# A first mixture layer whose last bias is added outside its products, with two dense token tiles in place of three, and blank products and earlier tables in the last layer

## The chip, the cores and the metric

The kernel runs on one core of a Trainium2 chip. The metric is the device time of one execution in microseconds (us). Three runs of the kernel before took 1397.26, 1397.58 and 1397.50 us, a median of 1397.5. The core has TensorE (PE in the profile; its weight loads are PEld), VectorE (DVE), ScalarE (ACT), GpSimd (POOL) and SyncE (SP), which issues most DMAs.

## The reference, cut to what matters

2048 tokens of 128 floats (8 sequences of 256, 16 tiles of 128 tokens) go through four pairs of an attention-like stage and a mixture-of-experts stage, with a layer norm after each. Two mixtures matter here. The first has 8 experts, and each token takes its 2 best:

```
gout = xt @ Wg.T; topv, topi = top_k(gout, 2); w = softmax(topv)
g = xt @ W1[e].T + b1[e];  v = xt @ W2[e].T + b2[e];  h = silu(g) * v       # 128 -> 256
eo = h @ W3[e].T + b3[e]                                                    # 256 -> 128
out = sum over e of comb[t, e] * eo[e, t];   x = layernorm(x + out)
```

The last runs four times over the tokens with one pool of 16 experts; each token takes one expert per round (`router` differs by round), and the result of a round is the input of the next:

```
logits = xt @ router; w = max(softmax(logits)); idx = argmax(logits)
out[t] = w[t] * (silu(xt[t] @ W1[idx[t]]) @ W2[idx[t]])                      # 128 -> 512 -> 128
```

All data is fp32. The bias `b3` takes part as the sum over e of `comb[t, e] * b3[e]`.

## The kernel before, in words

The program is a row of blocks, one per stage; each block has an instruction list for each engine, written out by hand in order, and semaphores (`Tally` counts) between them. A stage begins on all engines together when the one before is over on all of them. The order inside a queue is the order of the code.

**The first mixture, `moe_l0_stage` (L862), from 192 to 350 us of the span.** Its parts follow one another:

- SP issues the loads of all weights (L921, L922), of b3 (L923, one row of 8 x 128) and of the filters of the next stage. DVE finds each token's two experts, their weights, and for each (token, expert) pair a row in a buffer in DRAM that is sorted by expert. The first `DENSE` = 3 token tiles are left out of this; the other `SORTED` = 13 are sorted. DVE also builds `table`, which says for each of `PAIR_TILES` = 33 tiles of 128 pair rows where its expert's weights and bias lie and where its rows begin. It makes it by a diagonal that PE multiplies by ones (L985), and DVE casts the result (L1164, L1165).
- POOL scatters the sorted tokens into the pair rows: 2 x `SORTED` indirect DMAs (L966), one after the other.
- Meanwhile the three dense tiles go through all 8 experts (PE from L991, ACT L1058, DVE L1180 and L1188). A unit u is half of an expert's hidden width: two products with 384 columns (L994), `silu` on ACT, the gate on DVE (`m_inner`). After both halves PE makes, for each of the three tiles, a bias product (`k.ones[0:1]` by a row of b3, L1003) and two products with W3 into the same bank (L1005); DVE adds the result, scaled by `comb`, to `k.X`. PE has the sums of expert e behind the first half of expert e+1.
- SP waits until every scatter has landed (L926) and for the table, then loads pair tiles, up to `XRING` = 12 ahead (L934). Between them it issues four large zero fills of the last layer's row buffers (`clear_rows`, L1826, 2448 KB each), behind the 6th, 12th, 18th and 24th tile.
- The pair loop over 33 tiles. PE in step v: turns tile v (L1019); makes the 4 up products of tile v-1 (L1027); reads two registers from `table` (L1032 and L1034), and makes for tile v-3 the bias product (L1039) and two down products (L1041). ACT: reads a register (L1065), picks the expert's up weights of tile v (`m_up`, L1070) once `m_hT` of tile v-2 is made, two `silu` of tile v-1 (L1077), and writes tile v-3 out scaled (`m_ys`, L1085). DVE: copies the turned tile v (L1199), its destinations (L1202), then `m_hT` of tile v-2 (L1210). POOL scatters each tile to the two sums in DRAM (L972).
- SP loads the sums back in four groups (L941), and DVE adds both to `k.X` (L1219).

**The last mixture, `moe_l3_stage` (L1848), from 1025 us.** DVE finds the experts (L2149 on); PE starts with products of two "fold" banks (L1987), then counts (L2001 to L2003), and later the remaining banks; the folds turn W2 and the later routers into one matrix. POOL makes constants first (L1931 to L1947), then scatters 16 tiles (L1953). A round is a loop over 31 tiles like the pair loop. At its end PE makes `totals` (L2057), DVE `list_tiles` (L2113 on), PE spreads the table (`spread_table`, L1993), and SP begins to load the next round's tiles. At the start of each layer norm and of the first mixture PE runs 8 products of `k.blank` by the identity, 512 columns each (L126, L978), into a bank that nobody reads.

## Time and profile before

| | |
|---|---|
| Median of three runs | 1397.5 us |
| The profiled execution, its own time | 1397.07 us |
| Its span | 1395.3 us |
| Mean granted clock of TensorE | 0.87 of full speed |
| PE / PEld / DVE / ACT / POOL busy | 80% / 59% / 59% / 39% / 25% |
| DMA | 135.02 MB, mean 97 GB/s |

The span is the stretch from the first to the last instruction; the time has 1.8 us around it. A busy share says how long an engine had work in flight, not that it set the pace. In the timeline rows below, the first number is the start in us from the span's start, the second the time to the end of the last of the merged instructions, then engine, line, operation, output and inputs, the count, and in brackets the idle time before it and what ended that. Matmuls are pipelined: for their cost one reads from start to start. Each fp32 matmul has two records or more. In the rows of windows "PEclk" is the granted clock, 1.00 for 2.4 GHz and 0.50 for 1.2 GHz.

### The profile page before, as it was taken

How to read it: one execution, taken by the hardware profiler on the slowest of the kernel's cores; microseconds unless marked ns; L12 is line 12 of the kernel's file. 1: busy time of each engine (PE TensorE's matmuls, PEld its weight loads, DVE VectorE, ACT ScalarE, POOL GpSimd, SP SyncE). 2: the span in 40 equal slices, each digit the busy share in tenths (PEclk: the TensorE clock that was granted, in tenths of full speed). 3: DMA queues.
4: the chain of work that ended last, by engine and by line, in shares of the span. 5: the costliest groups of instructions: out<-in, count | busy, mean ns of one | idle time of the engine just before them, and what ended most of it. 6: DMA issues, size and time to landing. Idle time of an engine off the chain costs nothing. (4 is left out here: it accounts for less than half of the span.)

```text
span 1395.3 us, 31629 instructions
## 1 busy us (share of the span) xinstructions
PE 1111.8 (80%) x10680; PEld 817.0 (59%) x10680; DVE 823.7 (59%) x2873; ACT 546.6 (39%) x1175; POOL 343.3 (25%) x471
## 2 busy tenths in 40 slices
PE   8999889886887544789976856987698979789791
PEld 4655546775454531456644424553678969789791
DVE  6566163333588897745566885546853656656334
ACT  4456522454432001222222114322115757667581
POOL 3344325133100000000000015540033424424351
PEclk9999999998988557799997966999877989989896
DMA  2200646452000019238217065553902212021222
GB/s 52 53 25 3 241 171 248 159 196 67 1 3 3 4 37 374 85 82 177 38 40 257 2 201 133 145 114 124 301 21 64 56 35 59 24 65 44 50 52 62
DMA packets 112351, 135.02 MB, mean 97 GB/s; under 512 B 16795, under 2 KB 78316, under 8 KB 111539
## 3 DMA queue, kind: packets, MB, share of 16 engines
q1 hardware_dynamic: 99730, 118.48, 27.6%
q0 software_dynamic: 12464, 14.53, 4.1%
q8 instruction: 90, 1.47, 0.4%
q14 instruction: 67, 0.54, 0.1%
HBM read 67.13 MB, written 69.06 MB: 98 GB/s over the span
## 5 line engine op out<-in xcount | busy, mean ns | idle before, releaser
L2044 PE MATMUL m_psY<-large,m_hT 128*128 x992 | 141.5, 286 | 0.2
L2030 PE MATMUL m_psH<-m_xT,m_up 128*128 128x128 f32 x992 | 139.3, 286 | 0.0
L2030 PEld LDWEIGHTS m_psH<-m_xT,m_up 128*128 128x128 f32 x992 | 129.3, 203 | 0.0
L2044 PEld LDWEIGHTS m_psY<-large,m_hT 128*128 128x128 f32 x992 | 129.0, 194 | 0.5 <-issue 0.3
L1970 POOL DMA_INDIRECT rows<-m_ys,m_slot x93 | 90.5, 973 | 132.1 <-DVE m_slot L2238 119.7
L567 DVE TENSOR_REDUCE at_peaks<-at_ps 128x3 f32<-128x384 f32 x128 | 65.4, 551 | 47.8 <-PE at_ps L330 47.8
L2087 ACT ACTIVATE m_up<-large 128x512 f32 x124 | 78.0, 629 | 29.5 <-DVE m_valid L2141 17.2
L479 ACT ACTIVATE at_PT<-at_ps,at_bias 128x384 f32<-128x384 f32 x128 | 67.3, 577 | 50.3 <-PE at_ps L340 50.2
L1445 POOL IOTA sl_late<- 64x1024 f32 x2 | 2.0, 984 | 331.1 <-POOLq L682 331.1
L2096 ACT ACTIVATE m_hT<-m_psH 128x512 f32<-128x512 f32 x124 | 73.2, 590 | 20.6 <-PE m_psH L2030 20.4
L126 PE MATMUL ln_idle<-blank,ident 128*128 128x512 f32 x112 | 53.7, 635 | 26.2 <-PEq L883 13.5
L274 POOL TENSOR_SCALAR_AFFINE_SELECT at_PT<-at_PT 128x256 f32<-128x256 f32 x128 | 54.9, 430 | 74.1 <-ACT at_PT L479 70.2
L2108 ACT ACTIVATE m_ys<-m_psY,m_weight 128x144 f32<-128x144 f32 x124 | 47.3, 381 | 34.8 <-PE m_psY L2044 33.1
L126 PEld LDWEIGHTS ln_idle<-blank,ident 128*128 128x128 f32 x112 | 22.3, 205 | 53.2 <-issue 53.2
L972 POOL DMA_INDIRECT pair_sums<-m_ys,m_dest x33 | 32.4, 983 | 72.0 <-DVE m_dest L1202 55.0
L2019 PE MATMUL m_psX<-ident,m_xs 128*128 128x128 f32 x124 | 38.6, 311 | 14.3 <-DMA m_xs<-rows 13.0
L327 PE MATMUL at_ps<-large,at_QA 32*128 32x256 f32 x256 | 46.4, 437 | 3.5 <-ACT at_PT L479 2.3
L1342 ACT ACTIVATE pe_sg<-pe_psG 128x512 f32<-128x512 f32 x36 | 21.5, 597 | 69.6 <-PE pe_psU L1310 69.6
L1318 PEld LDWEIGHTS pe_psD<-m_wd,pe_hid 128*128 128x128 f32 x288 | 37.5, 191 | 18.7 <-DVE pe_hid L1363 13.8
L1664 PE MATMUL m_acc<-se_place,se_parts 128*128 128x512 bf16 x192 | 47.1, 399 | 0.0
L337 PE MATMUL at_ps<-at_QA,large 32*128 32x256 f32 x256 | 44.8, 425 | 2.5 <-ACT at_PT L479 2.3
L1357 DVE TENSOR_TENSOR pe_hu<-pe_psU,pe_sg 128x512 f32<-128x512 f32 x32 | 22.1, 691 | 35.8 <-ACT pe_sg L1342 35.8
(662 smaller groups left out, 2682.7 us busy)
## 6 DMA issues: line engine op xcount, KB each, us to landing
rows<-blank SPq DMA_DIRECT2D x16, 2448.0 KB, 15.2
m_xs<-rows SPq DMA_DIRECT2D x124, 76.5 KB, 1.9
pair_rows<-blank SPq DMA_DIRECT2D x1, 8320.0 KB, 25.8
large<-in_L_attn_firs SPq DMA_DIRECT2D x4, 2048.0 KB, 18.0
large<-comb_rows SPq DMA_DIRECT2D x64, 128.0 KB, 4.9
se_wu<-in_L_ffn_up SPq DMA_DIRECT2D x32, 192.0 KB, 2.6
W2T<-in_L_ffn_down_turned SPq DMA_DIRECT2D x1, 4096.0 KB, 12.6
large<-in_L_ffn_up SPq DMA_DIRECT2D x4, 1024.0 KB, 8.1
```

The lines of the kernel that those rows point to most:

```text
L126: nc.tensor.matmul(idle[:], k.ident[:], k.blank[:, 0:512], start=True, stop=True)
L274: nc.gpsimd.affine_select(out=diag(PT[:, v % PRING]), in_=diag(PT[:, v % PRING]), compare_op=ALU.is_ge, fill=0.0, base=0, pattern=[[0, 2], ...
L327: return nc.tensor.matmul(psS[:, u % TILES, P:CAUSAL], QA[rows, g, keys(b, 1)], KA[rows, g, b * SEQ:(b + 1) * SEQ], start=False, stop=True ...
L479: nc.scalar.activation(PT[:, v % PRING, :, :].rearrange("p x c -> p (x c)"), psT[:, v % TRING, 0:CAUSAL], ACT.Exp, bias=k.at_bias[:, v % H ...
L567: nc.vector.tensor_reduce(peaks[:, b % 2, n, :], psS[:, u % TILES, 0:CAUSAL].rearrange("p (x c) -> p x c", c=P), AX.X, ALU.max).then_inc(r ...
L1664: i = nc.tensor.matmul(acc[:, g, :], parts[:, j // 2 % 2, part, :], place[:, j // 2 % 2, g * 512:(g + 1) * 512], start=False, stop=True, s ...
L1970: pool.indirect_dma_start(k.rows[(layer + 1) % 2], bass.IndirectOffsetOnAxis(slot[:, q:q + 1], 0), ys[:, q, :], None, bounds_check=E3 * N ...
L2030: m = nc.tensor.matmul(psH[b][:, c * P:(c + 1) * P], up[b][:, c * P:(c + 1) * P], xT[b][:], start=True, stop=True)
L2044: m = nc.tensor.matmul(psY[b][:, 0:wide], hT[b][:, c * P:(c + 1) * P], k.W2[:, bass.ds(e + c * WIDE, wide)], start=(c == 0), stop=(c == C ...
L2087: nc.scalar.activation(up[b][:], k.W1[:, bass.ds(e, F3)], ACT.Copy).then_inc(picked.sem, 1)
L2096: nc.scalar.activation(hT[b][:], psH[b][:], ACT.Silu).then_inc(silu_done.sem, 1)
L2108: nc.scalar.activation(ys[:, q, 0:WIDE], psY[b][:, 0:WIDE], ACT.Copy, scale=weight[:, j % XRING:j % XRING + 1]).then_inc(y_out.sem, 1)
```

## The change

In the first mixture:

- `DENSE` is 2 and `SORTED` 14. The dense units have 256 columns, the pair tiles are 35, the scatters 28.
- The bias products (L1003, L1039) and the register reads for them (L1034) are gone; the down products start their banks themselves. `table` has three parts.
- b3 is laid out on the host as a [128, 1024] matrix: row (half, tile of 8, expert), column (tile of 8, d), b3 where both tiles are the same and zero elsewhere. Its load has 512 KB in place of 4 KB.
- `comb` holds all 16 tiles. PE turns it behind unit 1, ACT copies it out, and behind units 5, 8, 11 and 14 PE makes a product of 64 rows by 512 columns, whose result is the bias sum of four token tiles; DVE adds it to `k.X`. ACT's and DVE's copies of X for the scatter are waited for first.
- ACT runs a one-column `silu` behind the `exp`, before it waits for the weights.

In the last mixture:

- POOL makes two constants that DVE made, ahead of its other work; DVE starts its search on the logits in place of a copy, and copies them later, while it would wait for the counts.
- ACT runs a one-column `silu` behind the folds.
- PE runs 5 blank products (512 columns) behind the last fold bank, and between rounds 5 behind `totals` and 6 behind the spread table.

```diff
-DENSE = 3
+DENSE = 2
@@ moe_l0_stage
-    GROUPS = [range(DENSE, DENSE + 4)] + [range(t, t + 3) for t in range(DENSE + 4, T, 3)]
+    OFFERS = (5, 8, 11, 14)
+    GROUPS = [range(2, 6), range(6, 10), range(10, 13), range(13, 16)]
-        b3 = sb("b3", [1, E * D])
+        b3 = sb("b3", [P, 8 * D])
@@ block.tensor
                     for t in range(DENSE):
                         o = sums_of[d % 2][:, t * P:(t + 1) * P]
-                        nc.tensor.matmul(o, k.ones[0:1, :], b3[0:1, d * D:(d + 1) * D], start=True, stop=False)
                         for h in range(C):
                             m = nc.tensor.matmul(o, inner[:, (2 * d + h) % 4, t * P:(t + 1) * P],
-                                                 W3[...], start=False, stop=h == C - 1)
+                                                 W3[...], start=h == 0, stop=h == C - 1)
                     m.then_inc(summed.sem, 1)
+                if u == 1:
+                    pe.wait_ge(*mixed.at(1))
+                    nc.tensor.transpose(psC[:, 0:P], flat(comb), k.ident[:]).then_inc(mix_turned.sem, 1)
+                if u in OFFERS:
+                    g = OFFERS.index(u)
+                    pe.wait_ge(*mix_out.at(1))
+                    if g:
+                        pe.wait_ge(*taken.at(g))
+                    rows = slice(64 * (g // 2), 64 * (g // 2) + 64)
+                    nc.tensor.matmul(psC[:], combT[rows, :], b3[rows, g % 2 * 512:(g % 2 + 1) * 512],
+                                     start=True, stop=True).then_inc(offered.sem, 1)
...
-                    pe.reg_load(bias[j % 4], table[0:1, 2 * NT + j:2 * NT + j + 1])
-                    d = pe.snap(bias[j % 4], min_val=0, max_val=(E - 1) * D)
                     pe.wait_ge(*hid_done.at(j + 1))
                     if j >= 2:
                         pe.wait_ge(*y_out.at(j - 1))
-                    nc.tensor.matmul(psY[b][:, 0:D], k.ones[0:1, :], b3[0:1, bass.ds(d, D)], start=True, stop=False)
@@ block.scalar
             nc.scalar.activation(gap[:], gap[:], ACT.Exp).then_inc(exped.sem, 1)
+            nc.scalar.activation(hT[0][:, 0:1], k.ones[:, 0:1], ACT.Silu)
...
+                if u == 1:
+                    act.wait_ge(*mix_turned.at(1))
+                    nc.scalar.activation(combT[:], psC[:, 0:P], ACT.Copy).then_inc(mix_out.sem, 1)
@@ block.vector
+            dve.wait_ge(*rowed.at(3))
             dve.wait_ge(*w_in.at(16 * (2 * E + 1)))
...
+                if u in OFFERS:
+                    g = OFFERS.index(u)
+                    x = k.X[:, 4 * g:4 * g + 4, :]
+                    dve.wait_ge(*offered.at(g + 1))
+                    dve.drain()
+                    nc.vector.tensor_tensor(x, psC[:].rearrange("p (t d) -> p t d", d=D), x, ALU.add)\
+                        .then_inc(taken.sem, 1)
@@ moe_l3_stage
+            for t in (again_e, again_t):
+                nc.gpsimd.memset(t[:, :, 0:1], 0.0)
+                m = nc.gpsimd.memset(t[:, :, 1:], 1.0)
+            m.then_inc(made.sem, 1)
...
+            def keep_busy(products):
+                for i in range(products):
+                    nc.tensor.matmul(psX[:], k.ident[:], k.blank[:, 0:512], start=True, stop=True)
...
             for r in range(3, 8):
                 fold_bank(r)
+            keep_busy(5)
             pe.wait_ge(*folded_out.at(8))
...
                     nc.tensor.matmul(totals(layer + 1), ...).then_inc(counts.sem, 1)
+                    keep_busy(5)
                     spread_table(layer + 1)
+                    keep_busy(6)
@@ block.scalar
             act.wait_ge(*folded_out.at(8))
+            nc.scalar.activation(hT[0][:, 0:1], k.ones[:, 0:1], ACT.Silu)
@@ block.vector
-            L = first[:, :, D:WIDE]
-            nc.vector.tensor_copy(L, k.logits[:]).then_inc(rowed.sem, 1)
-            nc.vector.memset(edges[:, 0:1], 0.0)
-            nc.vector.memset(again_e[:], 1.0)
-            nc.vector.memset(again_t[:], 1.0)
-            dve.drain()
-            nc.vector.memset(again_e[:, :, 0:1], 0.0)
-            nc.vector.memset(again_t[:, :, 0:1], 0.0)
-            nc.vector.tensor_reduce(peak0[:], L, AX.X, ALU.max)
+            nc.vector.tensor_reduce(peak0[:], k.logits[:], AX.X, ALU.max)
...
+            dve.wait_ge(*made.at(1))
             nc.vector.tensor_tensor_scan(flat(steps[:]), flat(again_e[:]), flat(same[:]), 0.0, ALU.mult, ALU.add)
...
             nc.vector.tensor_tensor(prior0[:], upto[:], sel0[:], ALU.subtract).then_inc(counted.sem, 1)
+            nc.vector.tensor_copy(first[:, :, D:WIDE], k.logits[:]).then_inc(rowed.sem, 1)
+            nc.vector.memset(edges[:, 0:1], 0.0)
             dve.wait_ge(*counts.at(1))
```

## Rows read from the trace of the kernel before

**Rows 1.** The page, part 6: issues, count, KB each, median us to landing.
```profile
m_xs<-rows SPq DMA_DIRECT2D x124, 76.5 KB, 1.9
```
**Rows 2.** Windows of the pair loop, columns PE, PEld, DVE, ACT, POOL busy (count), PEclk, DMA.
```profile
279.00:288.00 9.00, 6.73 (x51) 5.81 (x50) 2.96 (x15) 4.77 (x13) 2.95 (x3) 1.00 0.97 327
303.30:329.50 26.20, 26.02 (x187) 22.60 (x187) 10.50 (x49) 17.73 (x51) 12.48 (x13) 1.00 0.16 45
```
**Rows 3.** Timeline of PE in the pair loop, first and last turn among them.
```profile
258.38 0.47 PE L1019 MATMUL m_psX<-ident,m_xs 128*128 128x128 f32 x1 [1.03 <-DVE X L1188]
...
316.80 0.27 PE L1019 MATMUL m_psX<-ident,m_xs 128*128 128x128 f32 x1
...
317.95 0.48 PE L1039 MATMUL m_psY<-m_b,ones 1*128 x2
318.35 0.71 PE L1041 MATMUL m_psY<-m_W,m_hT 128*128 x4
318.90 0.27 PE L1019 MATMUL m_psX<-ident,m_xs 128*128 128x128 f32 x1
...
329.52 0.27 PE L1019 MATMUL m_psX<-ident,m_xs 128*128 128x128 f32 x1
```
**Rows 4.** Timeline of DVE at the pair loop's end, `m_hT` of two tiles.
```profile
330.10 0.60 DVE L1210 SCALAR_TENSOR_TENSOR m_hT<-m_psH,m_up,m_sg 128x128 f32<-128x128 f32 x2
332.05 0.61 DVE L1210 SCALAR_TENSOR_TENSOR m_hT<-m_psH,m_up,m_sg 128x128 f32<-128x128 f32 x2 [1.35 <-ACT m_sg L1077]
```
**Rows 5.** Register reads by line in the pair loop: ns min/median/max, first and last start.
```profile
L1034 PEldq TENSOR_LOAD <-m_table x33: 295/303/1132, 264.4 to 334.9; - x33
...
L1065 ACTq TENSOR_LOAD <-m_table x31: 272/278/928, 261.5 to 329.7; - x31
```
**Rows 6.** Timeline of PE in the dense part.
```profile
212.35 0.48 PE L1003 MATMUL m_psX<-m_b,ones 1*128 1x128 f32 x2
212.77 0.71 PE L1005 MATMUL m_psX<-m_W,m_inner 128*128 128x128 f32 x4
...
221.28 1.46 PE L994 MATMUL m_psY<-XT,m_W 128*128 128x384 f32 x4
```
**Rows 7.** Timeline of PE: eight blank products at full clock, and from idle.
```profile
192.37 7.11 PE L978 MATMUL m_psX<-blank,ident 128*128 128x512 f32 x16 [0.30 <-PEq L71]
...
350.25 9.14 PE L126 MATMUL ln_idle<-blank,ident 128*128 128x512 f32 x16 [13.54 <-PEq L883]
```
**Rows 8.** The scatter by line; SP's first pair tiles; POOL's last store (timelines).
```profile
L966 POOL DMA_INDIRECT pair_rows<-m_first,m_slot x26: 954/958/1129, 201.9 to 233.6; - x26
...
236.60 4.80 SPq L934 DMA_DIRECT2D m_xs<-pair_rows  x6
...
337.95 0.98 POOL L972 DMA_INDIRECT pair_sums<-m_ys,m_dest  x1 [0.45 <-issue]
```
**Rows 9.** DVE's adds of the returned sums, by line.
```profile
L1219 DVE TENSOR_TENSOR X<-m_first,X x8: 558/559/693, 344.6 to 349.3; 128x384 f32<-128x384 f32 x6, 128x512 f32<-128x512 f32 x2
```
**Rows 10.** Timeline of PE at the start of the last mixture.
```profile
1031.14 0.41 PE L2001 MATMUL m_psC<-m_sel,m_tri 128*128 128x256 f16 x1
...
1058.43 0.45 PE L2019 MATMUL m_psX<-ident,m_xs 128*128 128x128 f32 x1 [4.05 <-DMA m_xs<-rows]
...
1064.75 0.27 PE L2019 MATMUL m_psX<-ident,m_xs 128*128 128x128 f32 x1
```
**Rows 11.** Between the first two rounds: timeline of PE, and the window.
```profile
1133.46 0.17 PE L2057 MATMUL m_psH<-m_prior,m_onesh 128*128 128x16 f16 x1
1136.79 0.78 PE L1993 MATMUL m_psH<-m_diag,ones 31*128 31x124 f32 x2 [3.16 <-DVE m_diag L2136]
1140.33 0.48 PE L2019 MATMUL m_psX<-ident,m_xs 128*128 128x128 f32 x1 [2.75 <-DMA m_xs<-rows]
...
1146.67 0.27 PE L2019 MATMUL m_psX<-ident,m_xs 128*128 128x128 f32 x1
...
1133.50:1146.70 13.20, 6.83 (x33) 6.19 (x33) 5.16 (x33) 3.72 (x9) 2.88 (x4) 0.61 0.24 54
```

52 lines of the change are left out of this document (30 added, 22 removed).

## The prediction

> **What bounds the kernel now.** I read the page first: PE is busy 80% of the span, and a tile of rows lands 1.9 us after SP issues it, in the median [rows 1]. Such shares average over stages, and the diff touches two of them, so I went to the timelines of these. In the first mixture's pair loop PE is busy 26.02 of 26.20 us between 303.3 and 329.5 [rows 2], and a tile takes 2.10 us from turn to turn (316.80 to 318.90), of which the bias product takes 0.40 (317.95 to 318.35) and the down products 0.55 [rows 3]. PE sets the pace there, but a second loop lies just under it. `m_hT` of one tile on DVE releases `m_up` on ACT, `silu` follows behind it, and this releases the next `m_hT`. At the loop's end, where DVE is seen to wait for ACT's `m_sg` and not for PE, two `m_hT` start 1.95 us apart (330.10, 332.05) [rows 4]. The reader is to see that 1.95 is the floor once PE is relieved. In 279 to 288, while a zero fill holds the DMA engines at 97%, PE is busy only 6.73 of 9.00 us [rows 2]: a read of a register from `table` then takes up to 1.13 us in place of 0.30, and PE has two per tile [rows 5].
>
> Before the pair loop two chains run side by side: the dense part on PE, and POOL's scatter, 26 issues from 201.9 to 233.6, one per 1.27 us, after which SP begins to load pair tiles at 236.60 [rows 8]. PE turns the first tile only at 258.38 [rows 3]. The dense part ends last, with 20 us of slack in the scatter.
>
> In the last mixture the start of each round is bound by a chain of DVE, PE's table product, SP and the first tile's landing, in which PE stands idle [rows 11].
>
> **The change part by part.** Times are of the profiled execution, 1397.07 us (span 1395.3 and 1.8 around it); it is 0.4 below the median 1397.5, which I add at the end.
>
> *Dense part.* For each expert and tile it loses a bias product of 0.42 us (212.35 to 212.77) [rows 6], and every third tile goes. What is left, from above: 16 units, each 2/3 of 1.46, is 15.6 us; 16 pairs of down products of 0.71 are 11.4 [rows 6]; four block products of 512 columns, each an eighth of 7.11, are 3.6; the slow clock at the start costs 2.0 as it does eight blank products (9.14 against 7.11) [rows 7]. With 2 us for the last expert's way through ACT and DVE (an estimate, two of their operations and PE's last sum) it is 34.6 at most, from 205.05, so 239.7; merged rows overlap, and I expect 238. The block products' additions on DVE lie beside PE's units, and so do the turn of `comb` and its copy.
>
> *Where the gain stops.* The scatter gets 2 issues more, 2.5 us, and DVE's search 14 tiles for 13, which I put at 0.15. SP begins at 239.25, and the first tile lands 1.9 later [rows 1]. The first turn is at 241.2, not 238. So the pair loop starts 17.2 us earlier, and what is late next is POOL, by 3 us. That covers 512 KB of b3 in place of 4 KB (if the weights were in just in time before, that costs the dense part at most 2 us) and the hoisted `silu` table load, which is worth nothing there either. If this cover is gone each microsecond counts; 0 to 3 us late is my bound.
>
> *Pair loop.* PE loses 0.40 and has 1.70 left, so DVE and ACT's 1.95 sets the pace, and only 0.15 of the 0.40 is cashed. There are 35 tiles: 34 steps of 1.95 are 66.3. The four zero fills now all run beside the loop (two before), since SP issues them behind its 6th to 24th load. They last some 9 us each, so 18 tiles meet one. PE's one register read of up to 1.13 fits under the 1.0 us of up products; ACT's of up to 0.93 [rows 5] hides less well under `m_ys`. I take 0.1 per tile, 2.0 in all; bounds are 0 and 18 x (0.93 - 0.28) = 12. The loop takes 68.3 from first to last turn, against 71.1 (258.38 to 329.52) [rows 3]: -2.8, for two tiles more.
>
> *Behind it.* From the last turn to POOL's last store it is 8.4 us (329.52 to 337.95) [rows 3, 8]. Three last tiles lose a bias product each there, 1.2, and some of the second register reads: -1.7. The returned sums are added 0.56 us per three tiles and half [rows 9]; one tile more is +0.4.
>
> First mixture: -17.2 - 2.8 - 1.7 + 0.4 = -21.3.
>
> *Last mixture, start.* DVE begins 1.1 us earlier, since a copy and four fills leave its way. But PE's counts at 1031.14 show no idle time before them: they stand behind two fold banks [rows 10]. The early start is worth nothing. POOL's fills delay its constants by some 0.8 us, which DVE's earlier arrival would meet; bounds -0.4 and +0.4.
>
> *Blank products.* Five of them at full clock take 4.4 us (7.11 / 8 each), six 5.3 [rows 7]. Between rounds they start at 1133.6, and the table product stands behind them: it runs at 1138.0 and not 1136.79 [rows 11]. It takes half as long at full clock, so the table is 0.8 late, hidden behind the stores SP waits for. The next six hold PE until 1143.5, though the first tile lands at 1140.3: 3.1 us late. In return the clock stays at 2.4 GHz (before, the granted clock was 0.61 over this window). From the first to the fourth turn it took 6.34 at 1.2 GHz [rows 11]; the same steps at 2.4, three turns and two groups of up products at 1.0 and one of down at 0.9 with the first tile's way through ACT, are 3.85. Net +3.1 - 2.5 = +0.6, three times: +1.8. At the stage's start five products follow the folds, which end at 1054.4 (1058.43 less PE's idle time, 4.05), from the slow clock: 6.5 us or so by the cold row [rows 7], so the first turn is at 1061 in place of 1058.43, and +2.6 - 2.5 leaves +0.1 (1058.43 to 1064.75 was 6.32) [rows 10]. Bounds of all four: -10 (no delay) and +9 (the clock gives nothing back before the fourth turn: 3 x 3.1).
>
> The trace measures the clock's gain by what PE does in the slow stretch, and finds 2.5 us. The Trainium skill ("TensorE: Matmul & The Clock Gate", Terms) prices it as slow time times one half. A mean of 0.61 over 13.2 us is 10.3 us at half speed, and the rule would give 5 us per round and not 2.5, so that the products would pay; but half of the slow time here PE waits for a transfer, which no clock shortens.
>
> **Sum.** -21.3 + 1.8 + 0.1 = -19.4: 1377.7 for the profiled execution, and 1378.1 against the median.
>
> **The rivals.**
>
> *A, the loop keeps PE's pace.* 34 steps at 2.10 and not 1.95, because releases between three engines don't line up: +5.1, 1383. For it: PE has only 0.25 us spare, and DVE takes the turned tile ahead of `m_hT` in its order. Against: the turn comes 0.8 us before `m_hT` in my schedule.
>
> *B, the dense part is last after all*, up to 3 us behind the scatter: 1381. For it: b3's 512 KB and two more waits in PE's order. Against: my sum is from above.
>
> *C, the blank products pay.* They are over when the first tile lands, or the later pipeline starts better filled: -10 on the sum's +1.9, so 1366. For it: PE idles 3 us on either side of the table. Against: 11 products are 9.7 us, and from 1133.6 to 1140.3 are 6.7.
>
> *D, slower than before: the clock falls in the pair loop.* With 0.25 us of idle time per tile PE may be granted 1.2 GHz. Its work of 1.70 is then 3.4 a tile, 1.45 over the floor, and 14 of 35 tiles at it eat the whole 19.4; all 34 give +49, 1427. Against: from 279 to 288 PE was busy three quarters and the granted clock stayed 1.00 [rows 2]; it will be busy 87%. The Trainium skill (same page, "A second HAM failure mode: psum-queue depth-cycling") says that short idles between groups of products can make the clock swing; the trace, with its 1.00 at 75%, does not show it in this loop.
>
> *E, the change does no more than shorten PE where nothing waits*: the first turn hardly moves, since SP's wait is on something I took for early (the fills or firs in the DMA queues). If only half of the 17.2 comes, it is 1387; with none of it, 1395. Against: SP's first load came 3 us behind the last scatter's issue, the time that one needs to land, which speaks for the scatter alone [rows 8].
>
> **How the numbers follow.** The forecast has 0.58 (1374 to 1381), A 0.16, B 0.08, C 0.10, D 0.04, E 0.04. The time is the forecast's, 1378. The range goes from 1371 (part of C, and the lower bound of the fills) to 1386 (A and B together, or a few us of the fills' upper bound). About 0.2% is what a measurement of this kernel can tell from no change. Only D gives slower: 0.03 slower and 0.01 same of it; 0.02 more for same where C's opposite (+9) and the fills' 12 meet. So 0.94 faster, 0.03 same, 0.03 slower.
>
> **What would show it.** Right: PE's last dense sum some 3 us before the first turn (L1019), and that at 241; POOL's 28 scatters without a gap; `m_hT` 1.95 to 2.0 apart in quiet windows with PE idle 0.25 a tile; the counts of the last mixture again straight behind the folds; six blank products over 3 us after the first tile of a round is in, the clock 1.00 throughout, and rounds 0.6 longer. Wrong: a pair loop above 2.1 us a tile, or at 0.50; a first turn before 240 or after 245; rounds that became shorter.

## The result and the profile after

After took 1389.9 us (median of 14 runs, 1381.7 to 1393.8), before beside it 1397.4 (14 runs, 1390.0 to 1403.1): ratio 0.9942, 95% interval 0.9922 to 0.9962. A second measurement at the study's end gave 1386.9 against 1395.3, ratio 0.992 (0.9885 to 0.9954). By these two the change makes the kernel 7.5 to 8.4 us faster (a third, under a condition told of below, gave 0.9967, 0.9924 to 1.001), where I had forecast 19.4, and the time lies above my range of 1371 to 1386. The profiled execution of after took 1385.98 us.

I cut each trace at the first `ln_stats` row (L92) of each layer norm, in us:

| stage, with the norm ahead of it | before | before again | after | after again | same first mixture (three products behind the table, below) |
|---|---|---|---|---|---|
| up to the first norm | 178.5 | 178.0 | 179.3 | 185.1 | 178.1 |
| first mixture | 171.7 | 171.5 | 156.8 | 157.9 | 152.6 |
| its first turn, from the norm | 79.8 | 79.9 | 64.2 | 64.2 | 62.5 |
| its first to last turn | 71.14 | 71.10 | 72.15 | 73.09 | 69.54 |
| last turn to the next norm | 20.7 | 20.5 | 20.4 | 20.6 | 20.6 |
| the attention-like stage behind it | 238.4 | 238.8 | 241.2 | 240.3 | 240.7 |
| third mixture | 190.9 | 189.7 | 185.4 | 186.2 | 185.9 |
| last mixture | 367.1 | 367.4 | 372.3 | 376.4 | 370.0 |

So the first mixture gave 14.9 us and the last took 5.2 back. Stages that the change doesn't touch went both ways.

**Ahead of the pair loop.** The timelines of PE, POOL (by line) and SP in after, to be read against [rows 3, 6, 8]:

```profile
238.82 1.16 PE L1007 MATMUL m_psD<-m_W,m_inner 128*128 128x128 f32 x8 [1.08 <-DVE m_inner L1194]
243.53 0.45 PE L1031 MATMUL m_psX<-ident,m_xs 128*128 128x128 f32 x1 [3.56 <-DMA m_xs<-pair_rows]
```
```profile
L969 POOL DMA_INDIRECT pair_rows<-m_first,m_slot x28: 954/958/1127, 204.3 to 238.6; - x28
```
```profile
241.63 4.44 SPq L937 DMA_DIRECT2D m_xs<-pair_rows  x6
246.13 1.61 SPq L1851 DMA_DIRECT2D rows<-blank  x1
248.23 7.51 SPq L937 DMA_DIRECT2D m_xs<-pair_rows  x6
255.79 0.45 SPq L1851 DMA_DIRECT2D rows<-blank  x1
```

PE has its last dense sum at 238.8 and idles 3.6 us for the tile; POOL's last scatter is out at 238.6, SP's first load 3.1 later. What bounds the start is now the scatter, as forecast. The reader should also see SP's order: six tiles, a fill of 2448 KB, six tiles.

The scatter itself starts late, 25.0 us behind the norm where before has 23.3. PE and DVE ahead of it:

```profile
193.16 8.72 PE L981 MATMUL m_psX<-blank,ident 128*128 128x512 f32 x16 [0.30 <-PEq L71]
202.09 0.28 DVE L1145 TENSOR_TENSOR m_at<-m_psC,m_e 128x112 f32<-128x112 f32 x1 [1.79 <-PE m_psC L986]
```

The eight blank products take 8.72 us in place of 7.11 [rows 7], the granted clock is 0.81 from 193.1 to 201.9, and DVE waits 1.79 us for the counts behind them (0.25 in before). The kernel of the last column has the same code up to here and takes 7.11 again. So these 1.6 us are the clock's and not the edit's.

**In the pair loop.** PE in a quiet stretch, then around the seventh tile, where the fill stands in front of the load:

```profile
296.08 0.27 PE L1031 MATMUL m_psX<-ident,m_xs 128*128 128x128 f32 x1
296.62 1.13 PE L1039 MATMUL m_psH<-m_xT,m_up 128*128 128x128 f32 x8 [0.28 <-issue]
297.59 0.61 PE L1050 MATMUL m_psY<-m_W,m_hT 128*128 x4
298.04 0.27 PE L1031 MATMUL m_psX<-ident,m_xs 128*128 128x128 f32 x1
```
```profile
254.11 0.71 PE L1050 MATMUL m_psY<-m_W,m_hT 128*128 x4
256.84 0.33 PE L1031 MATMUL m_psX<-ident,m_xs 128*128 128x128 f32 x1 [2.02 <-DMA m_xs<-pair_rows]
257.01 1.15 PE L1039 MATMUL m_psH<-m_xT,m_up 128*128 128x128 f32 x8
258.25 1.22 PE L1050 MATMUL m_psY<-m_W,m_hT 128*128 x4
259.26 0.42 PE L1031 MATMUL m_psX<-ident,m_xs 128*128 128x128 f32 x1
259.47 1.92 PE L1039 MATMUL m_psH<-m_xT,m_up 128*128 128x128 f32 x8
```

1.96 us a tile (296.08 to 298.04) with PE idle 0.28, for 2.10 before [rows 3]. But tile 7 comes 2.0 us late, and right behind this idle time the up products take 1.92 in place of 1.13: the clock has fallen. The windows (columns as in [rows 2]) say so, and one row each of the loads and of the waits shows what is late:

```profile
248.00:257.00 9.00, 5.90 (x42) 4.79 (x41) 2.79 (x12) 5.37 (x15) 2.69 (x3) 1.00 1.00 332
257.00:262.00 5.00, 4.91 (x29) 4.64 (x29) 1.76 (x9) 2.73 (x8) 1.26 (x2) 0.66 1.03 385
288.00:306.00 18.00, 14.19 (x112) 12.43 (x110) 8.37 (x35) 11.56 (x33) 7.88 (x9) 1.00 0.24 66
```
```profile
DMA to landing us min/median/max: 1.8/3.5/9.2
```
```profile
DVE m_dest L1223 <- DMA pair_sums<-m_ys,m_dest: 4.1, 4, 1.7
```

A pair tile lands up to 9.2 us after its issue, and DVE waits 4.1 us in all (four times, 1.7 at most) for stores of sums made eight tiles ago.

**Between rounds of the last mixture.** PE from the totals to the first turn, and the window, against [rows 11]:

```profile
1119.05 0.17 PE L2091 MATMUL m_psH<-m_prior,m_onesh 128*128 128x16 f16 x1
1119.07 4.54 PE L2027 MATMUL m_psX<-blank,ident 128*128 128x512 f32 x10
1123.54 0.48 PE L2022 MATMUL m_psH<-m_diag,ones 31*128 31x124 f32 x2
1123.95 5.42 PE L2027 MATMUL m_psX<-blank,ident 128*128 128x512 f32 x12
1129.21 0.27 PE L2053 MATMUL m_psX<-ident,m_xs 128*128 128x128 f32 x1
```
```profile
1119.05:1129.21 10.16, 10.16 (x28) 4.45 (x28) 3.67 (x26) 0.63 (x1) 2.60 (x3) 1.00 0.15 33
```

PE is busy without a gap for 10.16 us, where 6.87 had been enough for the tile to be in (1133.46 to 1140.33). In return the clock is 1.00 and the first to fourth turn takes 3.92 us, not 6.34. A round takes 83.2 to 83.4, before 81.9 to 82.2 (81.4 to 82.1 in before again).

### The profile page after: what moved, and what is told of

It reads as the page before. It is cut to its first block and busy times, and to the rows that moved or that the text cites. A ratio compares the mean times of both kernels' runs of the same rounds, so it can differ in the third digit from the quotient of the medians.

```text
span 1384.3 us, 31526 instructions
## 1 busy us (share of the span) xinstructions
PE 1112.4 (80%) x10645; PEld 808.7 (58%) x10645; DVE 827.5 (60%) x2871; ACT 548.3 (40%) x1186; POOL 346.9 (25%) x478
## 3 DMA queue, kind: packets, MB, share of 16 engines
q8 instruction: 90, 1.47, 0.5%
## 5 line engine op out<-in xcount | busy, mean ns | idle before, releaser
L2064 PE MATMUL m_psH<-m_xT,m_up 128*128 128x128 f32 x992 | 133.0, 277 | 0.0
L2064 PEld LDWEIGHTS m_psH<-m_xT,m_up 128*128 128x128 f32 x992 | 122.5, 194 | 0.2
L567 DVE TENSOR_REDUCE at_peaks<-at_ps 128x3 f32<-128x384 f32 x128 | 65.4, 552 | 47.5 <-PE at_ps L330 47.5
L1039 PE MATMUL m_psH<-m_xT,m_up 128*128 128x128 f32 x280 | 41.3, 293 | 9.5 <-issue 5.0
L1039 PEld LDWEIGHTS m_psH<-m_xT,m_up 128*128 128x128 f32 x280 | 36.1, 202 | 14.6 <-issue 9.2
```

What stands on the lines that cost most here:

```text
L567: nc.vector.tensor_reduce(peaks[:, b % 2, n, :], psS[:, u % TILES, 0:CAUSAL].rearrange("p (x c) -> p x c", c=P), AX.X, ALU.max).then_inc(r ...
L1039: m = nc.tensor.matmul(psH[b][:, c * P:(c + 1) * P], up[b][:, c * P:(c + 1) * P], xT[b][:], start=True, stop=True)
L2064: m = nc.tensor.matmul(psH[b][:, c * P:(c + 1) * P], up[b][:, c * P:(c + 1) * P], xT[b][:], start=True, stop=True)
```

## The experiments

My theory after the result: the zero fills cost the pair loop more than the 2.0 us I had given them, by late loads and late stores; the blank products cost more than they bring because eleven are too many; the rest is where the clock's slow stretches happen to fall. The first twelve kernels ran under a condition that the first pair of traces doesn't have: before took 1434 to 1435 us there, and ACT stood still in the dense part (see the last section). Each ratio is to before run beside it, but the first turn came 84 to 99 us behind the norm, so these ratios need not be those of the undisturbed kernel. The last six ran without it.

### One mixture's change alone

The kernel with the change in one of the two mixtures, the other as before.

> The kernel before with the first mixture of the change alone (dense tiles, block products, early silu table); the last mixture is that of before. Two questions. (a) Does the last mixture explain part of the miss? In the traces of before and after it took 367.1 and 372.3 us from norm to norm. Theory: the blank products cost 1.25 us per round and 1.4 at the start, so without them the rounds are 82.0 again (83.3 after) and the time is about 5 us below the kernel after, 1.0 us of clock phase at the start aside: ratio to before 0.990 (1383 against 1397). Rival, that the last mixture's loss is only the phase of the clock when the stage starts: rounds at 83 here too, and the same time as after, 0.9945. (b) The first mixture: 15 us shorter than in before by norm to norm (171.7 to 156.8), first to last turn 72.1 as in the kernel after and not the 68.3 I forecast; if 72.1 was chance in one trace it is 68 to 69 here.

> The kernel before with the change in the last mixture alone (five, five and six blank products, early table). The first mixture must take 171.7 us again. Theory: rounds of 83.3 us and 1.4 us more ahead of the first turn, +4 to +5 in all, ratio to before 1.003 (1401 to 1402). My forecast's own terms for it were +1.9 in all, ratio 1.0014. Rival (the blank products pay, and what the trace of after showed is a phase of the clock): rounds at or under 82.0 and a ratio of at most 1.000.

The first alone: ratio 0.9918 (0.9886 to 0.995), 1421.8 us against 1434.3. The last alone: 1.0023 (0.9999 to 1.0048). Their product is 0.9941, within the intervals of all three ratios of after. The last mixture's part costs 3.6 us by the medians, and by the interval anything from nothing to 7; I had forecast 1.9. Its rounds under this condition scatter by over 1 us (84.4, 84.7, 83.3 with the old rounds; 82.9, 83.8, 84.3 with the new), so here they say nothing. The first mixture alone has a loop of 67.95, near my 68.3: the first turn came late, so that two of the fills were through before it.

### No blank products in the last mixture

```
-            keep_busy(5)            # ahead of the first round
-                    keep_busy(5)    # ahead of the table product
-                    keep_busy(6)    # behind it
```

> The kernel after without any of the 11 + 5 blank products of the last mixture; the early table and the moved fills on DVE and POOL stay. Theory (blank products cost): between rounds PE's clock falls to half again, the first turn of a round comes 6.9 us behind the totals in place of 10.2 and the first to fourth turn takes 6.3 in place of 3.9; rounds 82.0 in place of 83.3; the first turn of the stage 33.5 after its start in place of 35.5. In all -4 to -5 against after: 1385, ratio to before 0.991. Rival (they pay elsewhere, by a pipeline that starts full): the part from the fourth turn to the next totals gets longer by more than the 0.9 that the head of the round gains, and the time is that of after or above, 1390. If the early table is worth nothing, this kernel and the one with the change in the first mixture alone have one time.

Ratio 0.9923 (0.9894 to 0.9952): between after's and the theory's 0.991, and the same as the kernel with the first mixture's change alone (0.9918), so the early table is worth nothing that intervals of 0.3% can tell. The totals come again 7.0 to 7.2 us ahead of the first turn, and the clock falls (0.59 from 1136.88 to 1143.9). Its rounds took 85.7, 83.7 and 83.5, not the 82.0 of the theory, under the condition in which the old rounds took 83.3 to 84.7 too:

```profile
1136.88 0.17 PE L2090 MATMUL m_psH<-m_prior,m_onesh 128*128 128x16 f16 x1
1140.48 0.78 PE L2022 MATMUL m_psH<-m_diag,ones 31*128 31x124 f32 x2 [3.43 <-issue]
1143.93 0.47 PE L2052 MATMUL m_psX<-ident,m_xs 128*128 128x128 f32 x1 [2.66 <-DMA m_xs<-rows]
```

### The zero fills: in pieces, behind the loop, in the next stage, doubled

In pieces, each fill cut in four, one behind every second tile's load:

```
-                if j % 6 == 5 and j < 24:
-                    clear_rows(k, sp, j // 6)
+                if j % 2 == 1 and j < 32:
+                    clear_rows(k, sp, j // 8, j // 2 % 4)     # a quarter of a fill
```

> The kernel after, each of the four zero fills that SP issues beside the first mixture's pair loop cut into four pieces, one behind every second pair tile's load. Theory (what the loop lost against my 68.3 is the fills in bulk, which keep the loads of rows and the stores of sums from landing): no load lands 9 us late, DVE's waits for stored sums go, first to last turn 68 to 69 us in place of 72.1, ratio to after 0.997. Rival 1 (the bytes count, not the bulk: the same 16 MB or so must pass beside the same loop): 71 to 72 again, and the stalls are only spread. Rival 2 (A of the forecast, releases between three engines don't line up): 2.0 to 2.1 us per tile also where no fill runs; the trace of after has 1.96 there, so I expect this one to fail.

> The kernel after, once more, as the yardstick of the three runs beside it. Chips differ: in the last four runs ACT stood still for some 20 us in the dense part (222.4 to 243.6 in one trace) and was late again in the last round of the last mixture, in both kernels, so that the kernel before took 1434 there and not 1397; where this is so the first turn of the first mixture comes 85 to 87 us behind the stage's start, in place of 64, and the pair loop finds its first eight tiles landed. Theory: where ACT doesn't stand still, first to last turn is 72 us again, with one late tile (the sixth to eighth) and DVE's waits for stored sums; rounds 83.3. Where it does, the loop is 66 and the rounds are 84 to 85. Ratio to before 0.994 either way. Rival (the 3.8 us of late tile and late stores were one execution's chance): 68 to 69 with no such wait on the undisturbed chip.

> The kernel after with the four zero fills issued behind the loads of the returned sums, none beside the pair loop. Theory (the fills are what the loop lost): 34 steps of 1.96, so 66.6 and at most 67.5 from first to last turn, no late tile, no DVE wait for stored sums; against 72.1 a gain of 4.5 to 5.5 in this stage. The fills then run beside the norm and the start of the next stage: bound 0 to 4 us of that back, since 1.5 us a fill is all that a transfer of the weights there could lose if it stood just behind one. Rival 1 (releases between three engines cost it, not the fills): 70 or more. Rival 2 (the loop is bound by ACT or DVE at 2.1 a tile, fills or no fills): 71 to 72.

> The kernel after with the four zero fills moved out of the first mixture into the scan of the stage behind it, where SP has nothing else to issue (its queue is empty from 350 to 530 us) and the DMA engines move 1 to 4 GB/s. The run with the fills behind the returned sums gave a pair loop of 65.4 us without one late step, but lost 8.4 us behind the loop, since SP needed 16.3 us to issue them and the stage's end waits for SP. Theory: the loop is 65.4 again (68.1 with the fills in the yardstick, 72.1 in the first trace of after), the part behind it 20.5 again, the scan unchanged: -2.7 to -6.7 against after, ratio to before 0.990 to 0.992 (after: 0.9942). Rival (the fills delay something in the scan or the gate, whose queue of fills stands behind them): the gain of the loop is paid back there and the time is that of after.

> The kernel after with the same four zero fills issued twice, so eight beside the pair loop, one behind every third tile's load from the third on. Only the cost of fills is asked. With none the loop from first to last turn took 65.4, with four 65.8 to 69.3 where the first of them was over before the loop began, and 72.1 where it was not. Theory (each fill beside the loop costs it 1 to 1.7 us by late loads, late stores of sums and slow register reads): 7 such fills, so 72 to 77. The DMA engines' time alone: eight fills are 72 us of all 16 engines, and the pair tiles' own traffic comes on top, so the upper end may be passed. Rival (a fill costs the loop next to nothing, what was lost came from elsewhere): 66 to 69.

First to last turn: pieces 65.77; after again 68.07 (the other kernels with its fills: 65.75, 67.75, 67.95 and 69.31); no fill beside the loop 65.38 (behind the returned sums) and 65.40 (in the next stage's scan); doubled 69.01. The steps of the loop without fills are 1.95 to 1.97 us from the fifth on, as my 1.95 had it; the whole is under 34 of them because the first two turns stand less than 1 us apart. So 65.4 is what ACT, DVE and PE need, and rival A, a loop that keeps PE's old pace, is out. Doubling added less than I wrote (69.0, not 72 to 77). At 9 us each, two of the eight were over before the late first turn, so six cost 3.6 us, 0.6 each. These are single traces: the same two fills inside the loop cost between 0.3 and 3.9 us in five kernels.

In time, the pieces gave 0.9926 (0.9896 to 0.9955) and the doubled fills 0.9976 (0.9945 to 1.0007), neither apart from after again's 0.9967 (0.9924 to 1.001). To move the fills away did not pay: 1.0008 (0.9967 to 1.0049) behind the sums, 0.9985 (0.996 to 1.0009) in the scan. Behind the sums, SP and DVE:

```profile
345.00 16.30 SPq L1851 DMA_DIRECT2D rows<-blank  x4
```
```profile
361.74 3.19 DVE L92 BATCH_NORM_STATS2 ln_stats<-X 128x6 f32<-128x128 f32 x16 [8.35 <-PEq L886]
```

The four issues last 16.3 us, the block ends only when SP is through, and the norm waits 8.35 us. In the scan, where SP and the DMA engines were idle, the rival held: the stage took 248.3, against 238.8 in after again and 238.3 to 243.3 in all kernels with this first mixture and no fills in the scan. PE at the same products, after again and then with the fills beside it:

```profile
392.29 1.30 PE L2445 MATMUL ds_psA<-de_kT 32*32 32x32 f32 x128 [1.92 <-issue]
395.74 1.93 PE L2445 MATMUL ds_psA<-de_kT 32*32 32x32 f32 x128 [2.15 <-issue]
```
```profile
389.09 1.93 PE L2448 MATMUL ds_psA<-de_kT 32*32 32x32 f32 x128 [4.92 <-issue]
394.46 1.93 PE L2448 MATMUL ds_psA<-de_kT 32*32 32x32 f32 x128 [3.44 <-issue]
```

After each 128 records (64 products of two records) PE waits with nothing that the profile shows to release it, 1.5 to 2.2 us in after again. Beside the fills it is 4.9 in the stop during which they keep the DMA engines full (1.03 from 384.0 to 389.1), 3.4 in the next (0.32) and 1.8 in the one after. The page's DMA queues list 90 packets of the instruction kind with 1.47 MB, 16 KB each, and such a packet starts just ahead of or in each of these stops. I read it as code that arrives later; that was not tested by itself.

### Where the fills fall into the loop, and the stores

```
-                if j % 6 == 5 and j < 24:        # behind tiles 5, 11, 17, 23
+                if j % 6 == 2 and j >= XRING:    # behind tiles 14, 20, 26, 32
-                    clear_rows(k, sp, j // 6)
+                    clear_rows(k, sp, j // 6 - 2)
```
and, for the second kernel, rings of 12 in place of 8 for `ys` and `dest`.

> The kernel after with its four zero fills behind the loads of the tiles 14, 20, 26 and 32 in place of 5, 11, 17 and 23. SP loads twelve tiles ahead without a wait, so that in the last runs, where the first turn came late, the fills behind 5 and 11 were over before the loop began; now all four fall into it. Theory (a fill inside the loop costs it 1.3 to 1.7 us: 2.7 over 65.4 with two inside, 6.7 over it with four in the first trace of after): 70.7 to 72.1 from first to last turn, four groups of late steps. Rival (in the first trace of after it was the early first turn, with the loads only just ahead of PE, and not the number of fills): 66 to 69 again.

> The kernel after with a ring of twelve result tiles in place of eight in the first mixture, fills as in after: DVE and ACT wait for the stored sums of twelve tiles ago. In the first trace of after DVE waited 4.1 us for them, four times, longest 1.7. Theory (late steps come from late stores of sums): no such wait, loop 65.8 to 66.5 against 67.8 to 69.3 in four traces of the same fills. Rival 1 (late loads and slow register reads make the late steps): 67.8 to 69.3 as before. In the time of the whole kernel either is too small to be seen.

These ran without ACT's stall, first turns 64.3 and 62.5 behind the norm. With all four fills in the loop but none at its start it took 67.83: the theory of 1.3 to 1.7 a fill fell, 0.6 is what a fill costs there. With the deeper rings the wait for stored sums is gone, and the loop took 68.47; the same fills with rings of eight gave 69.54, 72.15 and 73.09. The two steps that in those three traces are together 0.9 to 3.6 us over (the 22nd and 23rd) are 1.97 and 1.96 with the deeper rings. The seventh tile's step is 3.8 us there too, and 4.2, 3.9 and 4.3 in the three others; with the later fills no step is above 2.51. So the stores are worth 1 us or more, and the fill that SP puts in front of the seventh tile 2 us. A fall of the clock can come on top, and need not: behind this stop it fell in after, in after again and with the deeper rings, and did not in the fourth trace, nor behind single steps of 3.3 to 3.9 us elsewhere in these loops. Ratios 0.9918 (0.9885 to 0.995) and 0.9935 (0.9904 to 0.9965), not apart from after.

### Three blank products, and on which side of the table

```
-            keep_busy(5)                         +            keep_busy(3)
-                    keep_busy(5)                 +                    keep_busy(3)
                     spread_table(layer + 1)
-                    keep_busy(6)                 +                    keep_busy(3)
```

> The kernel after with three blank products in place of the five, five and six of the last mixture. Theory: at full clock three take 2.7 us, so in a round the table product stands at totals + 2.8 and PE is free at + 6.4, before the first tile lands at + 6.9; the first turn comes there and not 10.2 behind the totals. If the granted clock stays 1.0 until then, the first to fourth turn takes 3.9 (after) and not 6.3 (before): rounds of 80.0 to 81, 1.0 to 2.0 below those of before and 2.3 to 3.3 below after, 8 to 11 us in all with the start. Rival 1 (the clock falls all the same, since PE idles in two gaps of 1.5 us): 6.3 again and rounds of 82.0. Rival 2 (DVE gives it back: the part from the fourth turn to the totals was 0.5 longer in after, and DVE is busy without a gap there): rounds 81.5 to 82, whatever the head gains.

> The kernel after with three blank products at the last mixture's start, none ahead of a round's table product and three behind it. The table product comes at totals + 3.3 as in before, at 6.9 the first tile lands, and between stand 2.7 us of products. Theory (the clock needs PE busy on both sides of the table): it falls between the rounds, first to fourth turn 5.4 to 6.7, rounds 84 as without any product. Rival (three behind the table are enough, the 3 us of idle time ahead of it are not): first to fourth turn 4.0 to 4.6, rounds 81.5 to 82.5 as with three and three.

Three and three: 1420.1 us against 1434.9, ratio 0.9857 (0.9783 to 0.9932), after again beside it 0.9967 (0.9924 to 1.001). Rounds 82.3, 83.2, 82.0 for 84.7, 85.2, 84.5, that is 2.3 shorter each as the theory said. Rival 2 is out: the part from the fourth turn to the totals is the same in both (70.6, 71.2, 70.4 and 70.6, 71.0, 70.4). The first four turns took 4.1 to 4.7 us and not 3.9. None ahead and three behind: 0.9901 (0.9872 to 0.9931), rounds 82.0 to 82.2, first to fourth turn 3.9. The rival held, but for another reason than I gave:

```profile
1116.86 0.17 PE L2091 MATMUL m_psH<-m_prior,m_onesh 128*128 128x16 f16 x1
1120.46 0.79 PE L2022 MATMUL m_psH<-m_diag,ones 31*128 31x124 f32 x2 [3.43 <-DVE m_diag L2173]
1121.17 4.94 PE L2027 MATMUL m_psX<-blank,ident 128*128 128x512 f32 x6
1125.95 0.27 PE L2053 MATMUL m_psX<-ident,m_xs 128*128 128x128 f32 x1
```
```profile
1116.86:1125.95 9.09, 5.66 (x11) 2.56 (x12) 3.67 (x26) 0.63 (x1) 2.60 (x3) 0.62 0.14 35
```

PE idles 3.4 us, the clock falls (0.62 over the window), the three products run at half speed, 4.9 us in place of 2.8, and hold the tile up by 2 us; by their end the clock is back.

### One fold bank ahead of the counts; three dense tiles

> The kernel after with one fold bank ahead of the last mixture's counts in place of two; the second stands behind them with the rest. It asks what the early DVE start of the change is worth once PE no longer holds it. Theory: DVE has its flags 1.1 us earlier than in before, at some 4.8 us behind the block's start where the second fold bank ends at 5.9 to 7.0; the counts come 1.0 to 2.2 earlier, the table and SP's first load with them. But PE's remaining seven banks and the blank products take as long as before, and the first turn stands behind them: it moves by 0 to 0.3 us, and the time is that of after. Rival: the first turn waits for the tile and not for PE, and comes 1 to 2 us earlier.

> The kernel after with three dense token tiles as before, the block products kept: it parts the two edits of the first mixture. By the sum's prices the dense part is longer by a third of its units and down products (16 x 0.49 and 16 x 0.36, 13.5 us in all), the scatter shorter by two issues (2.5), the pair loop by two tiles (3.9), the sums added 0.4 less. Where ACT doesn't stand still the first turn then hangs on PE and comes 10 us later than after: the stage +6. Where ACT stands still for 20 us until the scatter is through (the last eight runs), the first turn moves by the share of the dense part that is left behind the stall, some two thirds of it, +9, and the stage by +5. Rival (the third dense tile costs nothing, the block products bring all of the gain): the stage as in after, or up to 4 us shorter.

One fold: ratio 0.9975 (0.9936 to 1.0014), no gain over after again's 0.9967. The counts come 1.7 us earlier (19.9 behind the norm for 21.6), but the folds end 2.5 later and the first turn 2.7 later. The early start of DVE can't be cashed in this order of PE's queue.

Three dense tiles with the block products kept: 0.9948 (0.9928 to 0.9969), as after. The first turn came 5.3 us later than in after again, the loop took 61.9 over 33 tiles, and the stage 174.8 for 176.1: the theory's +5 fell and the rival held. Where ACT stands still, the third dense tile costs what its two pair tiles save, and the block products bring the whole gain. Without the stall it wasn't tried.

### Both remedies

> Both remedies in one: the fills in the scan stage, and three blank products in place of five, five and six. Theory: the parts add up, since they lie in different stages: -2.7 to -6.7 from the pair loop and -8.0 from the last mixture (three rounds 2.3 each and 1.3 at the start, as measured in the run with three products): 11 to 15 us under after, ratio to before 0.984 to 0.987. Rival (the gain of the three products was clock chance): no more than the fills' part, 0.990 to 0.992, and rounds of 84.

> The kernel after with three blank products in each place and each fill in four pieces behind every second pair tile's load. Theory: the two add up, the loop at 65.8 (measured with the pieces) where bulk fills gave 67.8 to 69.3, and rounds of 82.3 with a start 1.3 shorter: 8 + 2 = 10 us under after, ratio to before 0.984 to 0.988. Rival (with the fills spread over the whole loop their last pieces run into the norm and the stage behind, which took 243.3 in that run against 240.8 as the mean of the others): 0.988 to 0.990, as with three products alone.

Fills in the scan and three products: 0.9902 (0.9865 to 0.994), the scan's loss again (246.9); the ratio is the rival's, but the rounds of 82.0 to 82.7 are not, so the three products' gain was no chance of the clock. Pieces and three products: 1373.2 us (1369.8 to 1377.1) against 1397.3, ratio 0.9826 (0.9795 to 0.9856), 14 to 17 us under after's two medians beside a before of nearly the same time, where the theory had 10, and the best kernel of the study. Its loop took 65.69 with an early first turn, a tile landed within 2.9 us at most, and its rounds took 80.3, 80.6 and 80.8:

```profile
1112.42 0.17 PE L2094 MATMUL m_psH<-m_prior,m_onesh 128*128 128x16 f16 x1
1112.45 2.82 PE L2030 MATMUL m_psX<-blank,ident 128*128 128x512 f32 x6
1116.02 0.48 PE L2025 MATMUL m_psH<-m_diag,ones 31*128 31x124 f32 x2 [0.75 <-DVE m_diag L2176]
1116.42 2.84 PE L2030 MATMUL m_psX<-blank,ident 128*128 128x512 f32 x6
1119.21 0.33 PE L2056 MATMUL m_psX<-ident,m_xs 128*128 128x128 f32 x1
```
```profile
1112.42:1123.80 11.38, 9.69 (x45) 5.68 (x45) 5.08 (x31) 3.50 (x9) 2.79 (x4) 1.00 0.22 49
```

The first turn comes 6.8 us behind the totals, as early as without a product, and from the totals to the fourth turn, the window's 11.38 us, the clock is 1.00; before took 13.2 for it (12.7 to 13.3 in before again).

### Both kernels again

> The kernel before once more, for a second trace of its stages. Theory: its first mixture takes 171.7 within 1 us, the stage behind it 237 to 239 and the last mixture 367.1 within 1 us with rounds of 82.0, so that the differences between the kernels in the last stage are the change's, and the -5.4 us in the second mixture a difference in where the clock stands at that stage's start. Rival (a kernel's own stages vary by 3 to 5 us from trace to trace): they scatter as widely as the two kernels differ, and no stage's difference under 3 us says anything.

> The kernel after once more, beside the kernel before on the same chip. Theory: the first mixture takes 151.5 to 153.5 as in the three later traces with an undisturbed ACT (the 156.8 of the first trace was its slow end), so 19 us less than before where I forecast 21.3; the last mixture 370 to 372, 3 to 5 more than before where I forecast 1.9 more; the stage behind the first mixture 2 to 3 more than before, where I forecast nothing. Rival: 156 to 157 again, the forecast's first term off by 6.

The first theory held: before repeats all its stages within 1.2 us (what the expectation calls the second mixture is the third of the table). The second fell: 157.9 for the first mixture, as the rival had it. This execution of after was its slowest (1398.5 where the others took 1378.9 to 1388.5), with slow stretches that the first trace hasn't. In the attention stage, ahead of anything that changed, after and after again:

```profile
48.00:63.00 15.00, 13.35 (x197) 8.27 (x195) 9.35 (x20) 8.36 (x17) 5.78 (x15) 1.00 0.04 12
```
```profile
48.00:63.00 15.00, 12.32 (x114) 7.61 (x110) 5.82 (x13) 4.65 (x9) 3.25 (x8) 0.54 0.01 3
```

and in its pair loop a second fall, again behind a stop:

```profile
293.70 0.27 PE L1031 MATMUL m_psX<-ident,m_xs 128*128 128x128 f32 x1
296.57 1.13 PE L1039 MATMUL m_psH<-m_xT,m_up 128*128 128x128 f32 x8 [2.60 <-ACT m_up L1083]
298.19 0.42 PE L1031 MATMUL m_psX<-ident,m_xs 128*128 128x128 f32 x1
298.54 2.05 PE L1039 MATMUL m_psH<-m_xT,m_up 128*128 128x128 f32 x8
```

## Why the prediction was wrong, point by point

**The first turn: right.** Forecast 17.2 us earlier, found 15.6 in both traces of after and 17.3 with the same first mixture in a third. PE's dense part ended 3 to 4 us ahead of the tile, the scatter bound it, as its step said. The 1.6 us between are the slower blank products ahead of the counts, for which the sum had no term.

**The pair loop: the step that failed.** I wrote -2.8 and it was +1.0 (72.15 against 71.14), +2.0 the second time. The floor was right: forecast 66.3, found 65.4. Mis-sized is the term of the zero fills, 2.0 us, which measured 4.1 to 7.7 (69.54, 72.15 and 73.09, less 65.4). I priced them by register reads alone. For fills that meet a loop well under way that was near: four of them cost 2.4 us (67.83 less 65.4). The runs showed three other ways: the fill in front of the seventh tile's load, 2 us (gone with later fills); stores that land late, for which DVE waits before it can write a destination, 1 us or more (gone with rings of 12); and the clock, which in three of four traces fell behind the first stop, 0.66 in 257 to 262 in after. The last is rival D in small: the two steps behind the stop take 2.4 us each, about 1 us in all, and not 49. [Rows 2] had shown the clock at 1.00 through a fill, and I took that for the rule. Before's own trace could have warned me: beside each of its two fills three steps take 2.7 to 3.2 us in place of 2.1, 2.5 us a fill, where I gave a fill 0.5. I had the bound of 12 in the text and gave it almost no room in the range.

**Behind the loop.** -0.3 for -1.3. POOL's last stores leave one per 1.29 us (321.07, 322.36, 323.65), so there POOL sets the pace and not PE, which lost its bias products. In before it did too, with one per 1.43 (336.52, 337.95).

**The last mixture: +5.2, forecast +1.9.** The two terms that I worked out were right: the first turn of a round came 3.1 us late in the mean (3.1), and the first four turns took 2.3 less (2.5). What I had at nothing made the difference: from the fourth turn to the next totals 69.1 to 69.3 us in place of 68.7, three times, 1.5 in all (68.9 to 69.4 in the other traces with the clock held up, 68.4 to 68.8 in before again); 0.9 ahead of the first round, and 0.7 from four small shortfalls in the first four turns. The norm and the folds took 2.0 us longer, as the clock fell sooner (0.94 over the norm, 0.50 over the first two folds, where before had 1.00 and 0.61), and the five blank products 5.6 us, 0.9 less than my 6.5. Why the part behind the fourth turn got longer isn't settled.

**Rival C was the right idea with the wrong number of products.** Three on each side are over when the tile lands and gain 1.1 to 1.5 us per round over the two traces of before. The rule that I weighed, slow time times one half (the Trainium skill, "TensorE: Matmul & The Clock Gate", Terms), gives 5 us a round. Measured were 2.4 from first to fourth turn in after, and 1.8 from totals to fourth turn in the best kernel (13.2 to 11.38). The traces don't agree with it here: of the 13.2 us PE is busy 6.83 [rows 11], and the rest no clock shortens.

**What nobody changed.** The stage behind the first mixture is 1.5 to 2.8 us longer in the two traces of after than in the two of before, the third mixture 3.5 to 5.5 shorter. The second repeats in every kernel with the change (184.1 to 187.0 without ACT's stall), the first not always (238.3 with the deeper rings). It may hang on where a stage's start meets the clock: over the same 95 us of the scan the granted clock is 0.51 in after and 0.55 in before. No experiment moved one stage's start alone, so this is only argued. The two nearly cancel.

**The account.** Missed were 6.4 us in the first mixture (1.6 ahead of the loop, 3.8 in it, 1.0 behind) and 3.3 in the last; the stages that nobody changed gave 1.4 back, so trace against trace it is 11.1 and not 19.4. The first trace of after was 4 us under its median, which makes 7.5. The largest single miss is the pair loop, and its largest part the term of the fills; the scatter's late start is the clock's. My range had room for one of these at a time, and for no scatter of a single kernel by some 15 us.

## What to carry to other kernels

A large transfer beside a loop is priced by what stands behind it in the queues, loads and stores both, and by the clock after each stop; cut it in pieces so that no load stands behind a long one. Blank products that hold the clock are worth it only up to the moment when the awaited tile lands: count the wait first and fill it to just under. And an idle queue in the next stage is not free: a block ends with its slowest queue, and PE's stops in the scan grew while the fills ran beside it, which I read, untested, as code that comes by the same DMA engines as the data.

## What the runs showed of the hardware

**ACT that stands still.** In the first twelve runs ACT and POOL in the dense part look like this (the first mixture's change alone):

```profile
222.43 0.47 ACT L1068 ACTIVATE m_share<-m_psH,m_W 128x256 f32<-128x256 f32 x1 [4.52 <-PE m_psY L997]
243.57 0.47 ACT L1068 ACTIVATE m_share<-m_psY,m_W 128x256 f32<-128x256 f32 x1 [20.66 <-remote]
```
```profile
238.10 0.96 POOL L969 DMA_INDIRECT pair_rows<-m_first,m_slot  x1 [0.30 <-issue]
```

PE's product for the second row was over by 221, and still ACT ran it at 243.57. In eleven of the twelve the standstill ended 4.7 to 5.6 us behind POOL's last scatter (1.8 in the twelfth), in kernels with 26 and with 28 of them (in the last mixture's change alone, and in that with three dense tiles, a second one followed it), and the last round of the last mixture took some 14 us more. Both kernels had it. The same chip ran the kernel before in 1434 us and some forty minutes later in 1397, so it isn't the chip alone, as I had supposed in an expectation; what it is stays open.

**A slow stretch comes and goes in one and the same kernel.** The windows at 48 to 63 us above differ by a granted clock of 1.00 and 0.54 with the same code ahead of them, and the first norm starts 5.8 us apart. At the fall after again has a wait that after hasn't, 1.94 us of PE for the transfer of `at_QA` (48.4 to 50.39); which of the two came first the traces don't settle. The Trainium skill ("TensorE: Matmul & The Clock Gate", Part 1) says that the number of slow products varies from run to run of one kernel; this pair of traces agrees. Such stretches are one reason why executions of after lie between 1379 and 1398 us; how much of that they make up isn't shown. A stage's length from one trace is good to a few us only.
